# Fused attention and recurrent layer on one core: the odd chunk's levels are made and turned two steps earlier

## The chip, the cores and the metric

The kernel runs on one core of a Trainium2 chip. The metric is the device time in microseconds of one execution. It was measured three times before the change: 699.0, 700.78 and 701.05 us, median 700.78 us.

## What is computed

The input is x of shape (2, 2048, 256), float32: 4096 tokens. The reference is a layer of attention with a hierarchical decay, a layer norm, and then an elementwise recurrent block with a second norm. Its attention part, cut to what matters here:

```python
dl  = (x @ Wdl.T).reshape(B, T, H, LV)              # H = 16 heads, LV = 12 levels
dt  = softplus(x @ Wdt.T + dt_bias)
Lam = softplus(Lp * dl)
cg  = cumsum(-exp(A_log) * dt, axis=1)
decay = exp(where(tril, cg[:, :, None] - cg[:, None], NEG))
lam_ts = Lam taken at level(t, s)                   # level = bit length of t XOR s
Wmat = (Q K^T / 8) * decay * lam_ts
o = (Wmat @ V) @ Wout.T + x ; o = layernorm(o) * ln_g + ln_b
x = layernorm(x + o)
c1 = step(c0, x[0]); c2 = step(c1, x[1])            # gated: f*c + i*g, over the two sequences
x = layernorm(x + tanh(x @ wo.T + c2 @ uo.T + bo))
```

## The kernel before

The 4096 tokens are cut into 32 chunks of 128 tokens, and two chunks make a pair (`sg`, 16 pairs). Everything is written by hand: each engine has its own instruction list, and all the lists walk over the same numbered steps, `STEPS = range(-3, NG + 13)`, with 4 steps to a chunk and so 8 steps to a pair. An engine works through its list strictly in the order in which it is written, and waits on semaphores. At each step an engine issues the jobs that belong to that step. The attention runs in the steps up to about 127 (545 us of the span), the recurrent block (`units_at`) behind it.

What belongs to a pair is scheduled by the table in `token_jobs(s)`: for an entry `(d, j)` the job `j` of pair `sg` falls on step `8 * sg + d - 11`. For the text below these are the jobs that matter, for chunk `ci = 2 * sg` (even) and `ci = 2 * sg + 1` (odd):

- Job 2, step `8 * sg - 10`: `softplus` on GpSimd (L1342), three tensor_tensor and two tensor_scalar over 128x416.
- Job 8, step `8 * sg - 8`: VectorE reads that result and makes `ng`, from which TensorE makes the cumulative sums in `decays`, two steps later.
- Jobs 5 and 7: `levels(sg, c)` on GpSimd (L1376), which writes `AT[c]` and `prod`; job 5 is the even chunk, job 7 the odd one. One step after each, VectorE's `turn_levels(ci)` (L1174) copies four levels into `C`, reduces `prod` into it and transposes `C` into `CT[c]`.
- At step `4 * ci` TensorE's `exponents(ci)` multiplies `AT` and `CT` into the exponents. It also waits until VectorE's `weights` of the chunk before have freed the banks.

Job 2, job 8 and job 7 belong to different pairs at one time: at step `8 * k` VectorE does job 8 for pair `k + 1`, while `exponents` of pair `k`'s odd chunk comes at step `8 * k + 4`.

Per chunk there is a second chain: `turn_y(ci)` (VectorE, L1035, step `4 * ci + 5`) adds the two parts of the result into `yt`, `out_proj(ci)` (TensorE, L501, step `4 * ci + 6`) multiplies it with the output weights, VectorE's `out_proj` (L1086) adds x and takes statistics, GpSimd's `root` (L1393, step `4 * ci + 7`) makes 1/sqrt, VectorE's `normalise` (L1098) and GpSimd's `x1` addition stand at step `4 * ci + 8`. `weights` (L993, tile `W`) multiplies scores and exponentials at steps 1 and 2 of a chunk.

Between these, TensorE runs the three-pass projections of the next pair (tiles `xH`, `xL`, `wH`, `wL`), one piece of 12 matmuls a step. Its list is the same before and after.

Of the kernel before, what the change touches and what calls it, by code (L numbers as in the profile page):

```python
# [45 lines left out]
def token_jobs(s):  # L46

    out = []
    for d, j in ((12, 7), (0, 0), (0, 1), (1, 2), (3, 8), (5, 3), (7, 4), (8, 5)):
        n = s + 11 - d  # L50
        if n % 8 == 0 and (0 if j == 7 else 1) <= n // 8 < NSG:
            out.append((n // 8, j))
    return out
# [16 lines left out]
def misc_jobs(s):  # L70

    out = []
    if 0 <= s < NG:
        ci, cc = s // 4, (s // 4) % CB
        if s % 4 == 0:
            out += [("keys", ci, 0), ("keys", ci, 1)]
        if s % 4 == 1 and cc:
            out += [("inter", ci, 0), ("inter", ci, 1)]
        if s % 4 == 3 and cc < CB - 1:
            out += [("state", ci, 0)]  # L80
    for sg, j in token_jobs(s):
        if j == 3:
            out += [("cgt", sg, 0)]
        if j == 5:
            out += [("cft", sg, 0)]
    for sg, j in token_jobs(s):
        if j == 0:
            out += [("tok", sg, 0), ("tok", sg, 1)]
    return out
# [61 lines left out]
def program(nc, x, xT, wqk, wtok, wout, wffn, cst, bcv, fv, out):  # L151
    ctx = ExitStack()
    with ctx:
# [222 lines left out]
        def _(e):  # L376
# [310 lines left out]
            for s in STEPS:  # L687
# [18 lines left out]
                for sg, j in token_jobs(s):  # L706
                    if j == 3:
                        decays(sg)
# [843 lines left out]
```

How the kernel before makes its waits and increments, by code:

```python
        @block.sync  # L299
# [11 lines left out]
            def load_coefs(sg):  # L311
                m, u = MISC["cft", sg, 0]
                e.wait_ge(m_free[m], u + 1)
                e.dma_start(scr.rearrange("a l c t -> (a l) (c t)"), cT[:, :]).then_inc(l_sc, 16)
                e.wait_ge(l_sc, 16 * sg + 16)
                for c in range(2):
                    ci = 2 * sg + c
                    if ci in INTER:
                        if ci >= 2 and ci - 2 in INTER:
                            for h in range(2):
                                m, u = MISC["inter", ci - 2, h]
                                e.wait_ge(m_free[m], u + 1)
                        for a in range(8):
                            e.dma_start(cB[c][16 * a:16 * a + 16, :, :, :].rearrange("p l u t -> p (l u) t"),
                                        scr[a, :, c, :].partition_broadcast(16)).then_inc(l_cB[c], 16)
# [8 lines left out]
                if i == 2:  # L335
                    e.dma_start(cs[:, :], cst[:, 0:C_CT]).then_inc(l_cst, 16)
                    load_xt(1)
            e.dma_start(C[:, :, :].rearrange("p h l -> p (h l)"), cst[:, C_CT:C_END]).then_inc(l_c, 16)
            e.dma_start(wo[:, :, :], kt(wout)).then_inc(l_wo, 16)
            load_x(0)
            e.dma_start(bv[:, B_G:B_END], bcv[:, B_G:B_END]).then_inc(l_b2, 16)
            e.dma_start(fvs[:, :], fv).then_inc(l_b2, 16)
            load_x(1)
            e.wait_ge(p_proj, 8)
            load_xt(2)
            for sg in range(NSG):
                load_coefs(sg)
```

## Time and profile before

| | before |
|---|---|
| runs, us | 699.0, 700.78, 701.05 (median 700.78) |
| the profiled execution's own time, us | 703.26 |
| its span, first to last instruction, us | 701.5 |
| TensorE busy | 670.3 us, 96% |
| VectorE busy | 475.2 us, 68% |
| GpSimd busy | 355.5 us, 51% |
| ScalarE busy | 339.6 us, 48% |
| mean granted TensorE clock | 0.98 |

Busy time is the time in which an engine had an instruction under way. The ends of matmuls are modelled. The idle time before an instruction is put down to the engine whose semaphore arrived last. The granted clock is the share of full speed (2.4 GHz) that TensorE was given; 0.50 is 1.2 GHz.

### The profile page before, as it was taken

To read this page: it belongs to the slowest core of one execution; us is meant where nothing else is said; L and a number is where in the kernel's file an instruction comes from. 1 tells how busy PE (TensorE), PEld (TensorE's weight loads), DVE (VectorE), ACT (ScalarE), POOL (GpSimd) and SP (SyncE) were. 2 spreads that over 40 slices of the span, in tenths; PEclk is the share of its full clock that TensorE was granted. 3 is DMA by queue.
4 is the path that set the end of the run, shared out by engine and by line. 5 is a ranking of instruction groups with operands and counts; after the bars stand their busy time and mean duration, and the time that the engine had idled before them with its cause. 6 is when DMAs were issued, how large, how long until landed. Compare 5 with 4: busy or idle time off the path is not lost.

```text
span 701.5 us, 22072 instructions
## 1 busy us (share of the span) xinstructions
PE 670.3 (96%) x9172; PEld 603.3 (86%) x9172; DVE 475.2 (68%) x1067; ACT 339.6 (48%) x759; POOL 355.5 (51%) x476
## 2 busy tenths in 40 slices
PE   5889999999999999999999999999997999999994
PEld 3779999998999999899999999999986788888894
DVE  2843768688776968675877769686877445454546
ACT  4545455544444453555444444545443434555555
POOL 1652755645564646466565636565464224344434
PEclk9989999999999999999999999999999899999997
DMA  8020312203050402112150503121222000000002
GB/s 296 26 57 18 80 40 58 68 31 96 3 95 7 92 21 78 35 33 64 35 95 3 95 9 90 35 63 49 35 66 93 1 1 0 31 32 31 30 31 91
DMA packets 53588, 37.09 MB, mean 53 GB/s; under 512 B 5360, under 2 KB 52080, under 8 KB 53488
## 3 DMA queue, kind: packets, MB, share of 16 engines
q1 hardware_dynamic: 53488, 35.67, 20.2%
q8 instruction: 73, 1.20, 0.7%
q14 instruction: 27, 0.22, 0.1%
HBM read 30.41 MB, written 5.24 MB: 51 GB/s over the span
## 4 chain that ended last, share of the span: by engine, by line
PE 88%; DVE 3%; DMA 2%; POOL 2%; ACT 2%; SPq 1%; issue 1%; DVEq 0%; ACTq 0%
PE bank L378 64%; PE bank L381 6%; PE bank L467 5%; PE bank L400 5%; PE bank L432 4%; PE bank L496 4%; SPq L325 1%; DMA xt<-in_wffn 1%; DMA bv<-in_bcv 1%; DVE t L966 1%; ACT t L735 1%; POOL wL L1333 1%; POOL t L1333 0%; DVE ng L963 0%; DVE t L963 0%
## 5 line engine op out<-in xcount | busy, mean ns | idle before, releaser
L378 PE MATMUL bank<-xH,wH 128*128 128x256 f32 x480 | 148.3, 309 | 2.4 <-ACT KT L735 1.1
L378 PE MATMUL bank<-xL,wH 128*128 128x256 f32 x480 | 136.1, 284 | 0.0
L378 PE MATMUL bank<-xH,wL 128*128 128x256 f32 x480 | 135.5, 282 | 0.0
L735 ACT ACTIVATE QT<-bank 128x512 f32<-128x512 f32 x64 | 38.2, 597 | 144.1 <-PE bank L378 144.1
L963 DVE TENSOR_TENSOR W<-bank,E 128x512 f32<-128x512 f32 x128 | 82.2, 684 | 35.6 <-PE bank L378 35.6
L378 PEld LDWEIGHTS bank<-xH,wH 128*128 128x128 f32 x480 | 91.4, 190 | 10.2 <-issue 9.0
L378 PEld LDWEIGHTS bank<-xL,wH 128*128 128x128 f32 x480 | 91.7, 191 | 0.4
L378 PEld LDWEIGHTS bank<-xH,wL 128*128 128x128 f32 x480 | 91.7, 191 | 0.0
L735 ACT ACTIVATE E<-bank 128x512 f32<-128x512 f32 x128 | 66.1, 603 | 17.4 <-PE bank L400 17.4
L378 PE MATMUL bank<-QT,KT 64*128 64x128 f32 x1024 | 65.9, 279 | 0.6 <-ACT E L735 0.6
L735 ACT ACTIVATE KT<-bank 128x512 f32<-128x512 f32 x64 | 38.0, 594 | 54.1 <-PE bank L378 54.0
L378 PEld LDWEIGHTS bank<-QT,KT 64*128 64x128 f32 x1024 | 59.7, 188 | 5.1 <-ACT E L735 0.8
L1333 POOL TENSOR_TENSOR lr<-mv,cs 128x1 f32<-128x1 f32 (+1 forms) x80 | 18.3, 229 | 80.8 <-DVE mv L1116 74.9
L1333 POOL TENSOR_TENSOR rs<-lr,cs 128x1 f32<-128x1 f32 (+1 forms) x80 | 52.4, 655 | 6.3
L1333 POOL TENSOR_TENSOR x<-oo,xs 128x256 f32<-128x256 f32 x32 | 23.5, 735 | 57.8 <-DVE oo L966 57.8
L1333 POOL TENSOR_TENSOR t<-t 128x416 f32<-128x416 f32 x45 | 49.8, 1107 | 3.6
L963 DVE TENSOR_TENSOR g<-g 128x512 f32<-128x512 f32 (+1 forms) x26 | 17.6, 678 | 37.5 <-ACT g L735 37.2
L400 PE MATMUL bank<-CT,AT 32*128 32x128 f32 x1024 | 38.7, 289 | 4.1 <-DVE CT L1188 4.1
L735 ACT ACTIVATE t<-t 128x416 f32<-128x416 f32 x64 | 35.3, 551 | 12.5 <-DVE t L1146 8.1
L1333 POOL TENSOR_TENSOR prod<-ll,cs 128x512 f32<-128x512 f32 x32 | 40.7, 1272 | 0.5 <-DVE ll L963 0.5
L378 PE MATMUL bank<-yH,wH 128*128 128x512 f32 (+1 forms) x102 | 39.8, 390 | 0.0
L400 PEld LDWEIGHTS bank<-CT,AT 32*128 32x128 f32 x1024 | 32.5, 192 | 8.3 <-DVE CT L1188 4.3
(149 smaller groups left out, 1660.5 us busy)
## 6 DMA issues: line engine op xcount, KB each, us to landing
cB<-scr SPq DMA_DIRECT2D x240, 64.0 KB, 3.0
xt<-in_xT SPq DMA_DIRECT2D x16, 256.0 KB, 3.7
xs<-in_x SPq DMA_DIRECT2D x16, 256.0 KB, 4.1
out<-xs SPq DMA_DIRECT2D x16, 256.0 KB, 2.1
xt<-in_wffn SPq DMA_DIRECT2D x8, 256.0 KB, 3.2
QT<-in_wqk SPq DMA_DIRECT2D x4, 256.0 KB, 5.8
KT<-in_wqk SPq DMA_DIRECT2D x4, 256.0 KB, 6.9
scr<-cT SPq DMA_DIRECT2D x16, 64.0 KB, 1.9
```

What stands on the lines that cost most here:

```text
L325: e.dma_start(cB[c][16 * a:16 * a + 16, :, :, :].rearrange("p l u t -> p (l u) t"), scr[a, :, c, :].partition_broadcast(16)).then_inc(l_cB ...
L378: return e.matmul(o, a, b, start=start, stop=stop)
L381: return e.transpose(o, i, ident)
L400: m = e.matmul(XP[q][:, :].rearrange("p (h t) -> p h t", h=H)[:, :, 8 * j:8 * j + 8], AT[b][r, j, :], CT[b][r, :].rearrange("p (h t) -> p ...
L432: y = e.matmul(YB[32 * n:32 * n + 32, 128 * k:128 * k + 128], V[sg % 3][:, c, v:v + 32], W[:, h, :], start=u == 0 and k == 0, stop=u == 1, ...
L467: t = e.matmul(MB[MISC["inter", ci, k][0]][32 * n:32 * n + 32, 128 * i:128 * i + 128], S[r, l, n, 16 * o:16 * o + 32], QT[b][r, 4 * o + n, ...
L496: t = e.matmul(MB[m][k:k + 64, 16 * q:16 * q + 16], Kt[:, 128 * q + k:128 * q + k + 64], Vw[b][:, c, 128 * h + 16 * q:128 * h + 16 * q + 1 ...
L735: return e.activation(o, i, f, **kw)
L963: return e.tensor_tensor(o, a, b, op)
L966: return e.scalar_tensor_tensor(out=o, in0=a, scalar=s, in1=b, op0=op0, op1=op1)
L1333: return e.tensor_tensor(o, a, b, op)
```

## The change

One number of the table moves: job 7 goes from step `8 * sg + 1` to step `8 * sg - 1`. GpSimd's `levels` for the odd chunk is issued there, and VectorE's `turn_levels`, always one step behind it, at step `8 * sg` in place of `8 * sg + 2`. No instruction is added or removed and no DMA moves; the lists of TensorE, ScalarE and SyncE stay as they were.

```diff
 def token_jobs(s):
 
     out = []
-    for d, j in ((12, 7), (0, 0), (0, 1), (1, 2), (3, 8), (5, 3), (7, 4), (8, 5)):
+    for d, j in ((10, 7), (0, 0), (0, 1), (1, 2), (3, 8), (5, 3), (7, 4), (8, 5)):
         n = s + 11 - d
```

First place: VectorE in the last pair that still has a job 8, around step 112. `t3<-pre,t3` is the first instruction of job 8, `oo` are the two of `normalise`, `yt` is `turn_y`. Before:

```order
L963 TENSOR_TENSOR S<-S 128x192
L1120 TENSOR_SCALAR xs<-x1,mv2,rs2 128x256
L966 SCALAR_TENSOR_TENSOR t3<-pre,t3 128x416
L963 TENSOR_TENSOR ng<-t3,eA 128x8x16
L1146 TENSOR_SCALAR t1<-t3 128x416
L1147 TENSOR_SCALAR t4<-pre 128x416
L966 SCALAR_TENSOR_TENSOR oo<-oo,mv1,bv 128x256
L966 SCALAR_TENSOR_TENSOR oo<-oo,rs1,bv 128x256
L963 TENSOR_TENSOR yt<-bank5,zs1 128x256
L963 TENSOR_TENSOR W<-bank1,E 128x512
```

The same place now:

```order
L1120 TENSOR_SCALAR xs<-x1,mv2,rs2 128x256
L1181 COPY C<-ll 128x16x4
L1183 TENSOR_REDUCE C<-prod 128x16x8
L1188 STREAM_TRANSPOSE CT1<-C 128x512
L966 SCALAR_TENSOR_TENSOR t3<-pre,t3 128x416
L963 TENSOR_TENSOR ng<-t3,eA 128x8x16
L1146 TENSOR_SCALAR t1<-t3 128x416
L1147 TENSOR_SCALAR t4<-pre 128x416
L966 SCALAR_TENSOR_TENSOR oo<-oo,mv1,bv 128x256
L966 SCALAR_TENSOR_TENSOR oo<-oo,rs1,bv 128x256
L963 TENSOR_TENSOR yt<-bank5,zs1 128x256
L963 TENSOR_TENSOR W<-bank1,E 128x512
```

The three instructions of `turn_levels` stood behind the chunk's last `W` before; they now stand ahead of job 8, `normalise`, `yt` and all four `W`.

Second place: GpSimd in the same step, as a piece of the difference. `lr1`, `rs1` are `root` of the inner norm, `x1` is the addition behind `normalise`; the five instructions of `softplus` stand directly ahead of this piece in both lists.

```order
 L1333 TENSOR_TENSOR lr1<-mv1,cs 128x1
 L1333 TENSOR_TENSOR rs1<-lr1,cs 128x1
-L1333 TENSOR_TENSOR x1<-oo,xs 128x256
-L1333 TENSOR_TENSOR AT1<-cs,cgt 128x512
-L1333 TENSOR_TENSOR prod<-ll,cs 128x512
+L1333 TENSOR_TENSOR AT1<-cs,cgt 128x512
+L1333 TENSOR_TENSOR prod<-ll,cs 128x512
+L1333 TENSOR_TENSOR x1<-oo,xs 128x256
 L1333 TENSOR_TENSOR lr2<-mv2,cs 128x1
```

`AT1` and `prod` pass the addition `x1` and stand directly behind `root`; `softplus` is still ahead of them.

Third place: the last pair, steps 119 to 121, on GpSimd, where the splits `wL` of the recurrent block's weights stand between.

```order
 L1333 TENSOR_TENSOR rs1<-lr1,cs 128x1
+L1333 TENSOR_TENSOR AT1<-cs,cgt 128x512
+L1333 TENSOR_TENSOR prod<-ll,cs 128x512
 L1333 TENSOR_TENSOR wL<-xt0,wH 128x2x256
 L1333 TENSOR_TENSOR x1<-oo,xs 128x256
 L1333 TENSOR_TENSOR wL<-xt1,wH 128x2x256
-L1333 TENSOR_TENSOR AT1<-cs,cgt 128x512
-L1333 TENSOR_TENSOR prod<-ll,cs 128x512
 L1333 TENSOR_TENSOR lr2<-mv2,cs 128x1
```

Here the two instructions pass two splits and `x1`.

## Rows read from the trace of the kernel before

**Rows 1.** The page: busy time of TensorE; the chain that ended last, by engine.

```profile
PE 670.3 (96%) x9172; PEld 603.3 (86%) x9172; DVE 475.2 (68%) x1067; ACT 339.6 (48%) x759; POOL 355.5 (51%) x476
PE 88%; DVE 3%; DMA 2%; POOL 2%; ACT 2%; SPq 1%; issue 1%; DVEq 0%; ACTq 0%
```

**Rows 2.** Waits, who waited for whom: us in total, times, longest us.

```profile
PE bank L400 <- DVE CT L1188: 4.1, 2, 3.8
PE bank L378 <- DVE ng L963: 3.1, 1, 3.1
...
DVE t L966 <- POOL t L1333: 32.4, 13, 7.9
```

**Rows 3.** Timeline of GpSimd, step 111 to 112: start us, us, instruction, idle time before.

```profile
489.29 3.59 POOL L1333 TENSOR_TENSOR t<-t 128x416 f32<-128x416 f32 x3
...
493.11 0.83 POOL L1333 TENSOR_TENSOR rs<-lr,cs 128x1 f32<-128x1 f32 x1
...
496.18 1.10 POOL L1333 TENSOR_TENSOR AT<-cs,cgt 128x512 f32<-128x512 f32 x1
497.22 1.27 POOL L1333 TENSOR_TENSOR prod<-ll,cs 128x512 f32<-128x512 f32 x1
```

**Rows 4.** Timeline of VectorE, steps 112 to 114.

```profile
492.91 0.59 DVE L966 SCALAR_TENSOR_TENSOR t<-pre,t 128x416 f32<-128x416 f32 x1 [1.04 <-POOL t L1333]
...
495.32 0.42 DVE L963 TENSOR_TENSOR yt<-bank,zs 128x256 f32<-128x256 f32 x1
...
500.46 0.18 DVE L1181 COPY C<-ll 128x64 f32<-128x64 f32 x1
...
501.91 0.39 DVE L963 TENSOR_TENSOR oo<-bank,xs 128x256 f32<-128x256 f32 x1
```

**Rows 5.** Timeline of TensorE, steps 114 and 116: out_proj and exponents.

```profile
497.90 1.03 PE L378 MATMUL bank<-wo,yt 128*128 128x256 f32 x4
...
503.82 1.17 PE L400 MATMUL bank<-CT,AT 32*128 32x128 f32 x32
```

**Rows 6.** Timelines, yt and out_proj of the pairs with the most and the least room.

```profile
271.19 0.42 DVE L963 TENSOR_TENSOR yt<-bank,zs 128x256 f32<-128x256 f32 x1
304.42 0.42 DVE L963 TENSOR_TENSOR yt<-bank,zs 128x256 f32<-128x256 f32 x1
...
274.19 1.03 PE L378 MATMUL bank<-wo,yt 128*128 128x256 f32 x4
306.13 1.03 PE L378 MATMUL bank<-wo,yt 128*128 128x256 f32 x4
```

**Rows 7.** Timelines of GpSimd and TensorE at the start, steps -1 to 2.

```profile
43.78 1.59 POOL L1333 TENSOR_TENSOR prod<-ll,cs 128x512 f32<-128x512 f32 x1
...
45.59 1.06 PE L378 MATMUL bank<-ng,cs 128*128 128x32 f32 x4 [3.05 <-DVE ng L963]
```

**Rows 8.** Timelines of GpSimd, VectorE and TensorE at the end, steps 119 to 124.

```profile
518.79 0.61 POOL L1333 TENSOR_TENSOR rs<-lr,cs 128x1 f32<-128x1 f32 x1
...
521.97 1.28 DVE L963 TENSOR_TENSOR W<-bank,E 128x512 f32<-128x512 f32 x2
524.18 1.02 DVE L963 TENSOR_TENSOR zt<-bank,cB 128x384 f32<-128x384 f32 x2 [0.94 <-PE bank L467]
...
530.03 1.89 PE L400 MATMUL bank<-CT,AT 32*128 32x128 f32 x32 [3.80 <-DVE CT L1188]
```

**Rows 9.** Stretches: us, then busy (instructions) of PE, PEld, DVE, ACT, POOL; PEclk, DMA share, GB/s.

```profile
45.62:55.86 10.24, 10.24 (x80) 9.76 (x84) 6.29 (x14) 2.75 (x5) 1.27 (x1) 0.50 0.01 2
530.31:533.73 3.42, 3.42 (x65) 2.72 (x61) 3.23 (x7) 0.14 (x1) 3.12 (x4) 0.50 0.31 91
690.74:694.15 3.41, 1.20 (x11) 0.99 (x9) 3.31 (x9) 2.82 (x7) 2.84 (x5) 1.00 0.26 88
694.15:697.57 3.42, 0.00 (x0) 0.00 (x0) 2.45 (x9) 2.70 (x7) 2.86 (x7) 0.50 0.33 111
20.50:21.80 1.30, 0.00 (x0) 0.03 (x1) 1.30 (x2) 0.55 (x1) 1.04 (x1) 1.00 0.00 0
```

## The prediction

> **What bounds the kernel now.** I read the page first. TensorE is busy 96% of the span and holds 88% of the chain that ended last, with VectorE at 3% and GpSimd at 2% [rows 1]. So a change on VectorE and GpSimd can only act through TensorE's waits, and the list of waits came next. There the turned levels, which this change moves, cost TensorE 4.1 us in 2 waits, of which one takes 3.8 us; and `ng` costs 3.1 us once [rows 2]. All that an earlier `CT` can remove is therefore 4.1 us. The reader should see the last line of that group too: VectorE itself waits 13 times, 32.4 us in all, for GpSimd's `t`, the end of `softplus`, and it does that exactly at the first instruction of job 8. That is the instruction ahead of which the change puts `turn_levels`.
>
> Then I read the timelines of one pair. GpSimd ends `softplus` at 489.29 + 3.59 = 492.88, makes `lr` and `rs` until 493.94, and only 2.2 us later `AT` and `prod` (496.18 to 498.49) [rows 3]. VectorE starts job 8 at 492.91, directly on `softplus`, ends `yt` at 495.74, and starts the turn at 500.46 [rows 4]. TensorE starts `out_proj`, which reads `yt`, at 497.90, so it has 2.16 us of room, and `exponents` at 503.82, some 1.9 us behind the end of the turn [rows 4, 5]. Nothing waits for `CT` in this pair.
>
> **The change, part by part.** Nothing is added; what matters is what now stands ahead of what.
>
> *The steady pairs.* VectorE's turn needs `prod`, and in GpSimd's list `prod` now stands behind `softplus` and `root`. The reading is: 492.88 (end of `softplus`) + 1.06 (`root`, 492.88 to 493.94) + 2.31 (`AT` and `prod`, 496.18 to 498.49) = 496.25 [rows 3]. VectorE picks it up some 0.04 us later, turns for 1.45 us (500.46 to 501.91) and so begins job 8 at 497.74, not 492.91. From there to the end of `yt` are 2.83 us (492.91 to 495.74), which gives 500.57, and 0.05 us for TensorE to notice: 500.62 [rows 4]. `out_proj` was due at 497.90 [rows 5]. So TensorE stalls for 2.72 us in this pair; put otherwise, `yt` comes 4.88 us later than before and the room of 2.16 us covers part of it. In the other direction, a `root` that runs beside an idle VectorE may take 0.8 rather than 1.06 us, and the shift is then 4.64 us.
>
> Such pairs are those of steps 8, 16, ..., 112: 14. I read `yt` and `out_proj` in each. The room goes from 1.29 us (304.84 to 306.13) to 2.58 us (271.61 to 274.19) [rows 6] (in two of the 14 VectorE comes to job 8 later than `softplus` ends, [rows 2] having 12 waits beside that of the start; one of them has 0.1 us less room, but is also shifted by less). Mean of the 14: 1.96 us. The stall is then between 4.64 - 1.96 = 2.68 and 4.88 - 1.96 = 2.92 us; I take 2.75, near the lower one because of those two pairs: 14 x 2.75 = 38.5 us, bounds 37.5 and 40.9 us. The single ones go from 2.1 to 3.6 us.
>
> Does the delay carry over from pair to pair, or vanish? `softplus` hangs on TensorE's `tokens`, which stands ahead of this `out_proj` in TensorE's list, so a late `out_proj` moves the next `softplus` by the same amount, and the stall comes anew each time. It doesn't grow either: relative to the late TensorE, VectorE is about 2 us behind at `yt`, and gets 1.45 us of that back at once since the turn no longer stands behind the last `W`. `exponents` needs these `W`: they ended at 500.46 before, and 502.5 in the late frame is still ahead of 503.82 [rows 4, 5]. On the queue of GpSimd `x1` is late with `normalise`, and the outer statistics on VectorE stand behind `W` anyway. No DMA and no SyncE work waits for any of it.
>
> *The start.* At step 0 the same happens to the first job 8. `prod` already ends at 43.78 + 1.59 = 45.37, since GpSimd runs ahead. VectorE turns until 46.86, and the two instructions of job 8 up to `ng` take 1.0 us: 47.9, where TensorE started at 45.59 [rows 7]. That is 2.3 us of longer wait. As a bound from below I take 1 us (the part of the slow clock that is then spent waiting), from above 4 us; value 2.
>
> *The end.* Here is what the change can win: the wait of 3.80 us for `CT` at 530.03 [rows 8]. The removed turn (1.45 us) stood directly ahead of it. But `exponents` also needs the last `W`, and VectorE gets to the first `W` later: `rs` ended at 519.40, `prod` (2.31 us) follows at 521.7, the turn at 523.2, `normalise` and `yt` take 1.3 us, so that `W` starts at 524.5 and not at 521.97 [rows 8]. VectorE had 0.94 us of idle time behind it, and loses the rest [rows 8]. 2.5 - 0.94 - 1.45 is about 0. Bounds: -1.5 us (all of the turn) and +1.5 us; value 0.
>
> *TensorE's clock.* The stalls have a second price. The granted clock was 0.50, which is 1.2 GHz, in a stretch of 10.24 us from 45.62 and in one of 3.42 us from 530.31, with TensorE at work in both [rows 9]. The first came behind a wait of 3.05 us, the second behind one of 3.80 us [rows 7, 8]. At the very end TensorE had no work for at most 2.2 us (1.20 us busy in 690.74:694.15) when the clock was 0.50 from 694.15 on. A gap of 1.30 us at 20.50 left the clock at 1.00 [rows 9]. The new stalls lie at 2.1 to 3.6 us, so between a length that did nothing and lengths that did. Half of a slow stretch is lost: 5.1 or 1.7 us. I take 5.1, because behind the first stood the same work as behind the new stalls (projections). For the number of stalls that bring the clock down the bounds are 0 and 14; I take 8, somewhat over half. 8 x 5.1 = 41 us; bounds 0 and 71 us.
>
> The Trainium skill, "TensorE: Matmul & The Clock Gate", section "Why this matters for your kernels", also wants idle gaps between bursts of matmuls avoided, but sets the harmful gap above most of the stalls worked out here. By that rule hardly any of them would bring the clock down, and this term would be near zero.
>
> *Sum.* 703.3 (the profiled execution's own time; its span is 701.5, with 1.8 around it) + 38.5 + 2 + 0 + 41 = 784.8 us. The median of the runs stands 2.5 us under the profiled one: 782 us.
>
> **The rivals.** *The stalls come, the clock holds.* For it: they are mostly shorter than the two waits that were followed by 0.50. Against it: the 2.2 us at the end. Up to 4 falls at 1.7 to 5.1 us belong to it. 703.3 + 38.5 + 2 - 2.5 = 741 us, up to 758. Chance 0.22.
>
> *The clock falls in nearly every pair, or stays down longer.* For it: the slow stretch behind 45.62 lasted until the next `exponents`, and behind the new stalls 5.9 us of full-speed work (497.90 to 503.82) [rows 5] stand ahead of the next `exponents`, 11.8 us at half speed, so that a fall could cost 6 us. 12 x 6 = 72: 703.3 + 38.5 + 2 + 72 - 2.5 = 813 us. Against it: the second fall was over after 3.42 us. Chance 0.15.
>
> *The other side, no stall at out_proj.* This needs `prod` to be there before `softplus` ends, so that VectorE turns in the 1.04 us in which it waits anyway [rows 4]. The place is GpSimd at step `8 * sg - 1`, and it decides whether the shift of `yt` stays under the room of 1.29 to 2.58 us. Then the kernel wins the 1.5 us at the end: 703.3 - 1.5 - 2.5 = 699 us. Against it: GpSimd's list has `softplus` ahead, and 13 times VectorE was already waiting for it [rows 2]. Chance 0.03, and 0.02 for a time within 0.3% of now, where the room would turn out larger than the rows say.
>
> *The change doesn't do what it says*: the two lists in the section on the change show both moves, so I give it nothing of its own.
>
> **How the numbers follow.** The forecast (stalls in all 14 pairs, clock down in 5 to 11 of them) has 0.58 and spans about 755 to 803 us; the held clock has 0.22, the heavier fall 0.15, the two without a stall 0.05. Slower by over 0.3% (what a measurement of this kernel can tell from no change) is 0.95, faster 0.03, same 0.02. The range leaves out the two stall-free cases and the upper part of the heavy one, and starts a little under the 741 of the held clock: 736 to 815 us.
>
> **What would show it.** Right: TensorE waits for VectorE's `yt` some 14 times, 2 to 3.6 us each, near 38 us in all; VectorE waits for GpSimd's `prod`, not `t`, at about 4.4 us a time; the turn starts directly behind it; the wait for `CT` is gone as a name, with `W` or nothing in its place; the start shows a wait of about 5 us for `ng`; the page's clock row has slices under 9, and the clock's mean is near 0.9. Wrong on the clock alone: a mean of 0.97 or more and a time near 741. Wrong altogether: no wait for `yt`, or waits under 1 us each, which would mean that `softplus` or `root` leave GpSimd earlier than I read, or that VectorE makes up for the delay ahead of `yt`.

## The result: 11% slower, and the profile after

The changed kernel takes 774.56 us (median of 6 runs, 772.42 to 777.45), the kernel before 700.91 us (6 runs). The ratio is 1.106, with a 95% interval of 1.102 to 1.109. The prediction said 782 us, between 736 and 815. The profiled executions compared below took 772.42 and 703.26 us of their own, so there are 69.2 us to explain in them.

The page after: busy time, and the granted clock in 40 slices.

```profile
PE 702.4 (91%) x9172; PEld 627.0 (81%) x9172; DVE 471.4 (61%) x1067; ACT 338.1 (44%) x759; POOL 352.5 (46%) x476
PEclk9989999999799999989898989899979789999998
...
PE 47%; POOL 12%; DVE 10%; ACT 3%; issue 3%; DMA 0%; DVEq 0%; POOLq 0%; ACTq 0%
```

TensorE's busy time went up by 32 us with the same matmuls, and the slices of the clock show why: several fell to 7 and 8 tenths. The chain that ended last can here be followed back only to 190.9 us, so its shares add up to 75% of the span. TensorE has 47 of these 75, where it had 88 of 99 [rows 1]. GpSimd and VectorE, 5% together before, have 22: in each of the ten steady pairs that the chain covers it runs through `softplus`, `prod` and the turn.

The waits after (who waited for whom: us in total, times, longest us), against [rows 2]:

```profile
PE bank L378 <- DVE yt L963: 34.7, 15, 3.1
PE bank L378 <- DVE W L963: 6.8, 1, 6.8
PE bank L378 <- DVE ng L963: 5.0, 1, 5.0
PE bank L378 <- DVE zt L963: 3.2, 6, 0.6
PE bank L400 <- DVE W L963: 2.0, 1, 2.0
...
PE bank L378 <- DVE zs L963: 0.6, 2, 0.4
...
DVE C L1181 <- POOL prod L1333: 79.5, 17, 10.2
```

The first line is new and the largest: 15 waits for `yt`, 14 of them in the steady pairs (33.2 us; the fifteenth, 1.5 us, is in the last pair). `ng` has gone from 3.1 to 5.0 us, and the 3.8 us for `CT` have become waits for `yt`, `zt` and `W`. VectorE no longer waits for `t` (32.4 us before) but for `prod`, for 79.5 us.

The same pair as in [rows 3 to 5], on GpSimd:

```profile
550.61 3.58 POOL L1333 TENSOR_TENSOR t<-t 128x416 f32<-128x416 f32 x3
554.15 0.18 POOL L1333 TENSOR_TENSOR lr<-mv,cs 128x1 f32<-128x1 f32 x1
554.41 0.57 POOL L1333 TENSOR_TENSOR rs<-lr,cs 128x1 f32<-128x1 f32 x1
554.95 1.09 POOL L1333 TENSOR_TENSOR AT<-cs,cgt 128x512 f32<-128x512 f32 x1
555.99 1.26 POOL L1333 TENSOR_TENSOR prod<-ll,cs 128x512 f32<-128x512 f32 x1
```

on VectorE:

```profile
557.28 0.20 DVE L1181 COPY C<-ll 128x64 f32<-128x64 f32 x1 [4.11 <-POOL prod L1333]
...
558.74 0.55 DVE L966 SCALAR_TENSOR_TENSOR t<-pre,t 128x416 f32<-128x416 f32 x1
...
561.10 0.42 DVE L963 TENSOR_TENSOR yt<-bank,zs 128x256 f32<-128x256 f32 x1
```

and on TensorE:

```profile
561.57 1.13 PE L378 MATMUL bank<-wo,yt 128*128 128x256 f32 x4 [2.18 <-DVE yt L963]
...
563.19 1.03 PE L378 MATMUL bank<-ng,cs 128*128 128x32 f32 x4 [0.48 <-DVE zt L963]
```

This is the sum of the prediction, link by link. `softplus` ends at 554.19, `prod` at 557.25 (3.06 us later, against 3.37 predicted: `root` is quicker beside an idle VectorE, which the prediction had as its lower bound), the turn takes 1.46 us, and `yt` ends at 561.52, 2.78 us behind the start of job 8 (2.83 predicted). `out_proj` waits 2.18 us, where 4.64 - 2.16 = 2.48 was the lower bound for this pair. The second wait, 0.48 us, was not foreseen: `decays` writes into a bank that `zt` still reads, and `zt` is late with `yt`.

Two stretches after show what the waits do to the clock (columns as in [rows 9]):

```profile
188.50:190.66 2.16, 0.94 (x4) 0.68 (x4) 2.12 (x5) 0.70 (x2) 0.72 (x1) 1.00 0.00 0
190.66:200.90 10.24, 9.95 (x73) 9.25 (x76) 7.21 (x20) 1.49 (x3) 3.31 (x6) 0.50 0.01 2
...
450.07:456.90 6.83, 6.70 (x32) 6.06 (x34) 5.98 (x16) 0.32 (x1) 1.30 (x3) 0.50 0.01 2
```

Behind the waits for `yt`, or already within them, the clock was at 0.50, that is 1.2 GHz, in 10 of the 14 pairs: three times for 3.4 us, five times for 6.8 and twice for 10.2. TensorE was at work for 62 us of these 65, so half of that, 31 us, was lost at first sight.

What the waits cost in all can be read from the starts of `out_proj`. These are its rows for chunk 0 and chunk 28, with the 14 steady pairs between them, first in the kernel before:

```profile
66.72 1.02 PE L378 MATMUL bank<-wo,yt 128*128 128x256 f32 x4
...
513.63 1.03 PE L378 MATMUL bank<-wo,yt 128*128 128x256 f32 x4
```

and in the changed one:

```profile
64.62 1.03 PE L378 MATMUL bank<-wo,yt 128*128 128x256 f32 x4
...
582.44 1.03 PE L378 MATMUL bank<-wo,yt 128*128 128x256 f32 x4
```

The 14 pairs took 446.9 us before and 517.8 us after, 70.9 us more. The stretch ahead of them was 2.1 us shorter in the execution after, and the stretch behind them 0.4 us longer, which gives the 69.2 us.

### The profile page after: what moved, and what is told of

Its sections match the earlier page's. It is cut to its first block, busy times and chain, and to the rows that moved or that the text cites. A ratio compares the mean times of both kernels' runs of the same rounds, so it can differ in the third digit from the quotient of the medians.

```text
span 770.6 us, 22072 instructions
## 1 busy us (share of the span) xinstructions
PE 702.4 (91%) x9172; PEld 627.0 (81%) x9172; DVE 471.4 (61%) x1067; ACT 338.1 (44%) x759; POOL 352.5 (46%) x476
## 4 chain that ended last, share of the span: by engine, by line
PE 47%; POOL 12%; DVE 10%; ACT 3%; issue 3%; DMA 0%; DVEq 0%; POOLq 0%; ACTq 0%
PE bank L378 37%; POOL t L1333 4%; PE bank L381 3%; ACT t L735 2%; PE bank L467 2%; PE bank L496 2%; POOL prod L1333 2%; PE bank L432 2%; POOL t L1346 2%; POOL t L1349 2%; PE bank L400 2%; POOL AT L1333 2%; DVE t L966 1%; DVE W L963 1%; DVE C L1183 1%
## 5 line engine op out<-in xcount | busy, mean ns | idle before, releaser
L378 PE MATMUL bank<-xH,wH 128*128 128x256 f32 x480 | 154.3, 321 | 2.4 <-ACT KT L735 1.1
L378 PE MATMUL bank<-xL,wH 128*128 128x256 f32 x480 | 141.3, 294 | 0.0
L378 PEld LDWEIGHTS bank<-xH,wH 128*128 128x128 f32 x480 | 97.2, 202 | 10.3 <-issue 9.0
L378 PEld LDWEIGHTS bank<-xL,wH 128*128 128x128 f32 x480 | 97.4, 203 | 0.4
L378 PEld LDWEIGHTS bank<-xH,wL 128*128 128x128 f32 x480 | 97.1, 202 | 0.0
L378 PE MATMUL bank<-wo,yt 128*128 128x256 f32 x128 | 40.0, 441 | 34.7 <-DVE yt L963 34.7
L378 PEld LDWEIGHTS bank<-wo,yt 128*128 128x128 f32 x128 | 25.6, 212 | 41.2 <-DVE yt L963 37.9
L1181 DVE COPY C<-ll 128x64 f32<-128x64 f32 x32 | 8.2, 256 | 79.5 <-POOL prod L1333 79.5
L1333 POOL TENSOR_TENSOR Vw<-V,dv 128x128 f32<-128x128 f32 x64 | 24.7, 416 | 39.7 <-ACT dv L735 39.7
L1333 POOL TENSOR_TENSOR xL<-xt,xH 128x512 fp32r<-128x512 f32 x15 | 19.3, 1287 | 49.8 <-ACT xH L735 49.8
```

What stands on the lines that cost most here:

```text
L378: return e.matmul(o, a, b, start=start, stop=stop)
L1181: e.tensor_copy(C[:, :, 24:28], ll[:, c, :].rearrange("p (h l) -> p h l", l=NL)[:, :, 4:8]).then_inc(d_own, 1)
L1333: return e.tensor_tensor(o, a, b, op)
```

## The experiments

**GpSimd's part alone, and job 8 ahead of the turn.** Which of the two engines' orders does it? The first kernel makes `AT` and `prod` early and turns them late:

```diff
-    for d, j in ((12, 7), ...
+    for d, j in ((10, 7), ...
-                for sg, j in token_jobs(s - 1):
-                    if j in (5, 7):
-                        turn_levels(2 * sg + (j - 5) // 2)
+                for sg, j in token_jobs(s - 1):
+                    if j == 5:
+                        turn_levels(2 * sg)
+                for sg, j in token_jobs(s - 3):
+                    if j == 7:
+                        turn_levels(2 * sg + 1)
```

> GpSimd's part of the change alone: AT and prod of the odd chunk are made at step 8k-1, and VectorE's turn stays behind the last W (step 8k+2). My theory (the whole loss comes from yt, which stands behind the turn and so behind prod, on VectorE): 701 us, within 2, TensorE waits for yt never, clock 0.98. Rival (GpSimd's order itself does the harm: x1 now stands behind AT and prod, the outer norm and its statistics come late): TensorE or VectorE waits for x or mv in each of 14 pairs, 710 us or more, up to 774.

Measured: 710.65 us (ratio 1.012, 1.010 to 1.014). My 701 was wrong, and so was the rival's mechanism: neither TensorE nor VectorE waits for `x1` or its statistics. TensorE's waits:

```profile
PE bank L378 <- DVE zt L963: 2.2, 6, 0.5
PE bank L378 <- DVE zs L963: 2.1, 6, 0.4
...
PE bank L378 <- DVE yt L963: 1.0, 2, 0.5
```

VectorE's and GpSimd's timelines in the pair of [rows 3 and 4] show the cause:

```profile
501.17 0.37 DVE L1146 TENSOR_SCALAR t<-t 128x416 f32<-128x416 f32 x1
501.45 1.26 DVE L1147 TENSOR_SCALAR t<-pre 128x416 f32<-128x416 f32 x1
502.63 1.48 DVE L966 SCALAR_TENSOR_TENSOR oo<-oo,mv,bv 128x256 f32<-128x256 f32 x1
504.15 0.48 DVE L966 SCALAR_TENSOR_TENSOR oo<-oo,rs,bv 128x256 f32<-128x256 f32 x1
```

```profile
501.23 1.25 POOL L1336 TENSOR_TENSOR AT<-cs,cgt 128x512 f32<-128x512 f32 x1
502.44 1.39 POOL L1336 TENSOR_TENSOR prod<-ll,cs 128x512 f32<-128x512 f32 x1
```

While GpSimd makes `AT` and `prod`, two VectorE instructions take 1.26 and 1.48 us in place of 0.37 and 0.48: the two engines hinder each other, and `yt` comes 1.9 us later behind the start of job 8 than before. Within this kernel L1147 took 1.27 us the 13 times that it ran beside `AT` or `prod` and 0.36 us the three times that it did not. Before, GpSimd did this work beside `W`, `zt` and `zs`. `W` and `zt` did not suffer; `zs` took 1.08 us in place of 0.43, where nothing waited for it. The late `yt` itself costs TensorE little, since most pairs have 1.8 us of room or more. What costs is `zt` and `zs` behind it, for which `decays` waits: of the 10.4 us that the 14 pairs are longer, 8.3 us lie between an odd chunk's `out_proj` and the next even one. The Trainium skill, "GPSIMD Engine Reference", section "Specifications", says that the two share their SBUF interfaces, with contention where a VectorE instruction has two SBUF inputs or runs in its 2-port mode. These rows agree as far as they go: L966 and `zs`, with two SBUF inputs, were slowed, and `W` and `zt`, which read a PSUM bank and one SBUF tile, were not; in which mode L1147, with one input, ran, no trace shows. In the changed kernel this cost is hidden, because VectorE stands still in these microseconds.

The second kernel is the changed one with `turn_levels` of the odd chunk moved behind `tokens` (job 8), still ahead of `normalise`:

```diff
                 for sg, j in token_jobs(s):
                     tokens(sg, j)
+                for sg, j in token_jobs(s - 1):
+                    if j == 7:
+                        turn_levels(2 * sg + 1)
                 if (ci := chunk_at(s, 8)) is not None:
                     normalise(ci)
```

> As the changed kernel, but in the same step VectorE does job 8 (1.5 us) ahead of the turn, in the time in which it would wait for prod. My theory: yt comes 1.5 us earlier than in the changed kernel, so the wait of TensorE for yt falls from 2.4 to 0.9 us a pair (12 us in all), some 4 us of waits for zt stay, the wait for ng at the start is 3 us again, and waits of 0.9 us leave the clock at 1.00: 717 us. Rival (any stall at this place brings the clock down, whatever its length): the same waits and 31 us of slow clock, 748 us. Rival (the harm is that ng comes late, not yt): 701 us.

Measured: 738.1 us (1.054, 1.048 to 1.060), 21 us above my 717.

```profile
PE bank L378 <- DVE yt L963: 22.1, 15, 2.2
...
PE bank L378 <- DVE zt L963: 3.7, 7, 0.6
PE bank L378 <- DVE ng L963: 3.1, 1, 3.1
PE bank L378 <- DVE zs L963: 2.1, 6, 0.4
```

`ng` is on time and half of the loss is still there, so it is not a late `ng` that counts but `yt`, and `zt` and `zs` behind it. The waits for `yt` in the steady pairs are 1.5 us each, not 0.9. Job 8 now runs beside `root`, `AT` and `prod` and slows them:

```profile
523.61 1.39 POOL L1336 TENSOR_TENSOR prod<-ll,cs 128x512 f32<-128x512 f32 x1
```

Here `prod` ends 3.62 us behind `softplus` (521.38), in the changed kernel 3.06 us. (L1147 took 1.27 us here too, but VectorE then stood still for 1.15 us until `prod` was there, so that cost nothing.) The clock stayed up in 12 of the 14. It fell in two pairs, behind waits of only 1.31 and 1.29 us, each followed by 0.49 us for `zt`, while the longest wait, 2.19 us, left it alone.

**The waits filled.** How much of the loss is the clock? The changed kernel and the kernel before got 14 more matmuls ahead of `out_proj`:

```diff
             def out_proj(ci):
+                if ci % 2 and 1 <= ci <= 27:
+                    e.wait_ge(a_qk, 8 * ((ci + 1) // 2 + 1) + 3)
+                    for _ in range(14):
+                        mm(banks[0][:, 0:256], wtH[:, 0, 0:128], wtH[:, 0, 0:256])
                 e.wait_ge(d_yt, ci + 1)
```

> The changed kernel with TensorE kept at work in its stalls: ahead of the odd chunks' out_proj in the 14 steady pairs it does 14 more matmuls of 128x256 (1.7 us in all, results never read) into the bank of the projections, once ScalarE has emptied it (about 0.8 us). My theory (the changed kernel loses some 37 us in waits and some 30 us by the clock that falls behind them): the waits are filled, the clock stays near 1.00 in the steady pairs, 743 us, up to 748 where the work is longer than the stall. Rival (the clock costs nothing of its own, since slow stretches only use up room that TensorE has): 774 us or a little more.

> The kernel before with the same 14 more matmuls at the same place, 14 times. There they fill no stall: each costs 1.7 us and about 0.8 us of waiting for ScalarE, 2.5 us x 14 = 35 us, 736 us, clock 0.98. It is the price of delaying out_proj by about as much as the change does, at full clock. If it comes near the filled changed kernel, the delay and the clock are all that the change does. A rival in which the shifted order on VectorE and GpSimd costs by itself has the filled changed kernel 10 us or more above it.

Measured: 772.11 us (1.099, 1.096 to 1.102) for the changed kernel, 737.57 us (1.052, 1.049 to 1.054) for the kernel before. The control came as expected: 36 us for 14 delays of 2.6 us at full clock, and no new fall of the clock in the steady pairs. The changed kernel stayed 34.5 us above it, which by the expectation would speak for a cost of the shifted order by itself; but this run did not test what it should:

```profile
PE bank L378 <- ACT QT L739: 26.9, 14, 2.6
```

The added matmuls waited 2 us for ScalarE themselves, so the gap stayed open and the work came on top. ScalarE's copy of `QT` stands behind its own part of job 8 (`Ln` of `t`), which waits for VectorE:

```profile
561.27 0.55 ACT L739 ACTIVATE t<-t 128x416 f32<-128x416 f32 x1 [4.72 <-DVE t L1150]
561.73 0.58 ACT L739 ACTIVATE QT<-bank 128x512 f32<-128x512 f32 x1
```

That is a second way by which a late job 8 reaches TensorE, hidden behind `yt` in the changed kernel. The rival's number was met for a reason that is not the rival's.

So the work was put where it waits for nothing, 18 matmuls (2.1 us) ahead of the projection one step earlier:

```diff
                 e.wait_ge(a_qk, 8 * sg + j)
+                if j == 2 and sg >= 2:
+                    for _ in range(18):
+                        mm(banks[0][:, 0:256], wtH[:, 0, 0:128], wtH[:, 0, 0:256])
```

> The changed kernel with 18 more matmuls of 128x256 (2.1 us, results overwritten) ahead of the projection of step 8k+1 in the 14 steady pairs, so that TensorE reaches the late out_proj 2.1 us later and waits there for 0.2 to 1 us only; unlike in the first filled kernel the added work waits for nothing of ScalarE. My theory (about 40 us of the change's cost are waits, about 30 us the slow clock behind them): the delay of yt stays, the clock stays at 1.00 in the steady pairs, 744 us, within 5. Rival (the slow clock costs nothing, since the next wait takes up what it loses): 774 us.

Measured: 751.31 us (1.071, 1.066 to 1.076): more work, and 23 us less time, though 7 us above my 744, because the delay is longer than the 40 us that I had put. Waits, and the steady pairs in one stretch:

```profile
PE bank L378 <- DVE yt L966: 5.1, 8, 1.5
...
PE bank L378 <- DVE zt L966: 3.6, 7, 0.6
PE bank L378 <- DVE zs L966: 2.1, 6, 0.4
```

```profile
60.00:572.00 512.00, 498.68 (x7917) 453.27 (x7915) 349.22 (x811) 226.58 (x537) 257.37 (x346) 1.00 0.20 48
```

The changed kernel, in the same stretch:

```profile
60.00:572.00 512.00, 472.51 (x7151) 428.19 (x7133) 333.80 (x781) 212.09 (x502) 245.84 (x329) 0.94 0.20 45
```

The clock was 1.00 in the steady pairs, and the delay stayed. Its size is read again from `out_proj` of the chunks 0 and 28:

```profile
67.50 1.02 PE L378 MATMUL bank<-wo,yt 128*128 128x256 f32 x4
...
560.54 1.03 PE L378 MATMUL bank<-wo,yt 128*128 128x256 f32 x4
```

The 14 pairs took 493.0 us, 46.1 us more than before and 24.8 us less than in the changed kernel. So 46 us are the delay at full clock and 25 us the clock, not quite the 31 of the halved stretches (the medians of the runs differ by 23.3 us). Pair by pair, the two kernels agree within 0.05 us in the four pairs in which the changed kernel's clock held. In the other ten a slow stretch of 3.4 us cost it 1.0 to 1.5 us, one of 6.8 us 2.3 to 2.7 us, and one of 10.2 us 4.2 or 4.3 us. One reason that it is less than half is in the waits: for `zt` and `zs` they are 5.7 us here against 3.8, so a slow clock uses up some room that TensorE else waits out.

**Is it the turn, or the prod it waits for?** Here the turn stays first in step `8 * k`, but `prod` has two buffers, and GpSimd makes both chunks' levels ahead of `softplus`:

```diff
-        prod = sb1("prod", [P, H, 8, 4])
+        prod = [sb1(f"prod{i}", [P, H, 8, 4]) for i in range(2)]
...
-                    if j in (5, 7):
-                        levels(sg, (j - 5) // 2)
+                    if j == 5:
+                        levels(sg, 0)
+                        levels(sg, 1)
...
```

(Chunk 1's levels are made ahead of the loop, and the waits for `prod` are adapted.)

> VectorE's turn stays where the change puts it, first in step 8k, but prod has a buffer for each chunk, and GpSimd makes both chunks' AT and prod at step 8k-3, ahead of softplus. My theory (the harm is the wait for a prod that stands behind softplus, 4.4 us a pair; the turn's own 1.45 us fit into the 1 to 3 us in which VectorE waits for softplus anyway): TensorE waits for yt in no pair or for tenths, 702 us, within 3. Rival (the 1.45 us of the turn ahead of job 8 do the harm): 14 stalls of 1.4 us or more, 725 us or more. A cost I can't see from here: AT and prod beside VectorE's work at step 8k-3 may slow that by about 1 us a pair, which would show as a later softplus, up to 710 us.

Measured: 701.41 us, ratio 1.001 (0.999 to 1.004): the whole loss is gone with VectorE's order as the change has it, the clock held in all 14 pairs, and they took 1.4 us longer than before. VectorE waits 9 times for `softplus` and not 13 times as in [rows 2], which fits a turn that fills some of that time:

```profile
DVE t L966 <- POOL t L1333: 14.1, 9, 5.2
```

**The two ends apart.** The table has both entries for job 7, and one pair takes the new one:

```diff
-    for d, j in ((12, 7), (0, 0), ...
+    for d, j in ((12, 7), (10, 7), (0, 0), ...
-        if ... (0 if j == 7 else 1) <= n // 8 < NSG:
+        if ... (0 if j == 7 else 1) <= n // 8 < NSG and (j != 7 or (d == 10) == (n // 8 == 15)):
```

> The change in the last pair alone (k = 15, steps 119 and 120). In the changed kernel the waits at this place came to 4.0 us (yt 1.5, zt 0.5, W 2.0) where the kernel before has 3.8 (CT) and 0.6 (E). My theory: the removed turn is paid back by the later W, 701 us, within 1.5. Rival (the earlier CT does win its 1.5 to 3.8 us here): 697 to 699 us.

> In the last pair GpSimd makes AT and prod at step 119 as in the changed kernel, but VectorE turns them behind the first two W of chunk 30 (step 121), where it had 0.94 us of idle time in the kernel before. My theory: of the 1.45 us of the turn 0.9 disappear in that gap, so exponents start some 0.9 us earlier; with a wait of 2.9 us in place of 3.8 us the clock may also stay up, which gives 1.7 us more. 699.5 us, between 698 and 701. Rival (AT and prod beside normalise slow VectorE by 1.9 us as in the kernel with GpSimd's part alone, and eat it): 701 us or more.

> The change in the first pair alone (k = 0, steps -1 and 0). In the changed kernel the wait for ng there was 5.0 us in place of 3.1 us, and the slow clock began inside that wait. My theory: 1.9 us more waiting, 0 to 2.7 us less slow clock at work: 701 us, within 2. Rival (the start belongs to the loss with 3 to 4 us of its own, since a longer wait brings a longer slow stretch): 704 us or more.

(The second has `turn_levels` of the last chunk behind the first two `W` of chunk 30, the third has 0 in place of 15.) Measured: the last pair alone has ratio 0.9998 (0.998 to 1.002), the variant in the gap 1.0004 (0.999 to 1.002), the first pair alone 1.0038 (1.002 to 1.006), 2.7 us. So nothing is won at the end, by either way, and my 699.5 for the gap was wrong where its rival was right: in the last-pair kernel `exponents` waited 2.20 us for `W` behind 1.5 us for `yt` and 0.5 for `zt`; in the gap variant `AT` and `prod` ran beside `normalise`, whose two instructions took 1.47 and 1.38 us, and ate the gap. At the start the interval is 1.1 to 4.2 us, against the 1.9 us by which the wait for `ng` is longer in the changed kernel; whether it costs more than this wait is not shown.

**A version of the kernel before with an earlier first `prod`.** The start has the same hindrance in the kernel before: job 8 ran beside `AT` and `prod`, 2.7 us up to `ng`.

```diff
             decayed_values(0)
+            levels(0, 1)
             for s in STEPS:
```

(with two `prod` buffers, and chunk 1 left out of job 7.)

> The kernel before with one thing changed: GpSimd makes AT and prod of chunk 1 ahead of the first softplus of the loop, where it waits 3.4 us for ScalarE, into a second prod buffer; VectorE's order is that of the kernel before. My theory: job 8 at the start no longer runs beside AT and prod, so that VectorE's two instructions up to ng take 1.0 us and not 2.7 us, TensorE waits 1.3 us and not 3.1 us for ng (as in the kernel with a second prod), 699.3 us, and up to 3 us less where the clock then stays up. Rival (softplus comes later by the 2.4 us of AT and prod): 701 us or more.

Measured: 700.81 us, ratio 0.998 (0.996 to 0.9994). It is the fastest kernel of the study, by 0.2%, at the edge of what the runs can tell: 0.4 to 2.9 us, in which the 1.8 us of the shorter wait for `ng` lie.

```profile
41.80 0.59 DVE L966 SCALAR_TENSOR_TENSOR t<-pre,t 128x416 f32<-128x416 f32 x1 [7.93 <-POOL t L1333]
42.43 0.37 DVE L963 TENSOR_TENSOR ng<-t,eA 128x128 f32<-128x128 f32 x1
```

TensorE waited 1.3 us for `ng`, not 3.1 us. The clock fell all the same, for 6.8 us.

## Why the prediction was right, and where its sizes were off

**The mechanism** held in the steps that it had, and lacked one path (below): `prod` behind `softplus` on GpSimd, the turn behind `prod`, job 8, `normalise` and `yt` behind the turn, and one stall of `out_proj` per pair that does not add up from pair to pair. The kernel with two `prod` buffers shows that the wait for `prod` is the cause; the same 1.45 us of the turn at the same place cost nothing without it.

**The stalls**: predicted 38.5 us, measured 33.2 us of idle time shown (14 waits of 1.80 to 3.09 us, mean 2.37). A part of the difference is in how waits are shown: matmuls of a projection start every 0.12 us but are drawn 0.28 us long, so that a gap behind them appears 0.16 us shorter than it is. By the starts of `out_proj`, the odd one came 35.5 us later behind the even one, summed over the 14 pairs. Most of the remaining 3 us is the quicker `root`.

**A term that was missing**: the prediction follows the delay on VectorE to `yt`, `W`, `x1` and the statistics, but not to `zt` and `zs`, which stand behind `yt`. It hits `decays` too, through the bank that they read: 8 waits, 3.8 us as shown. At full clock, in the filled kernel, the stretch from an odd `out_proj` to the next even one grew by 10.2 us over the 14 pairs, and 9.2 us of that is `decays`, which starts up to 0.8 us later behind `out_proj`. So the prediction's nothing was 10 us.

**The clock**: predicted 41 us from 8 falls of 5.1 us. There were 10 falls, but TensorE's work in them was 6.2 us each (31 us in all when halved), and the filled kernel puts the real price at 25 us, 2.5 us a fall. The step that was mis-sized is taking the 10.24 us stretch of [rows 9] as the typical one: it was the longest kind, two of ten. The prediction cites the Trainium skill, "TensorE: Matmul & The Clock Gate", section "Why this matters for your kernels", which wants no idle gaps above some 3 us between bursts of matmuls. The trace does not agree that shorter ones are safe: the waits of 2.5 to 3.1 us brought the clock down in 7 of 7 pairs, six of them with waits under 2.8 us, and those of 1.8 to 2.2 us in 3 of 7.

**The start**: 2 us predicted, 2.7 us (1.1 to 4.2) measured for it alone. In the two profiled executions compared here the changed kernel was even 2.1 us ahead at the first `out_proj`, because two things at the start were shorter: its first wait for `W` (6.8 us, before 8.5) and its slow stretch (6.8 us, with 4.85 us of work in it, against the 10.24 us of [rows 9]). **The end**: 0 predicted, 0 measured; the removed wait for `CT` turned into waits for `yt`, `zt` and `W` of 4.0 us in all.

The sum of what was measured between the profiled executions: 35.5 for `yt`, 10.2 for `decays`, 24.8 for the clock, -2.1 for the start and 0.4 for the end, 68.8 of the 69.2 us. Of the predicted 81.5 us the clock had 16 too many and `decays` 10 too few. That the time came within 8 us of the forecast is thus in part luck: two wrong sizes stood against each other.

## What to carry to other kernels

Moving a producer and its consumer "two steps sooner" gives slack only if the resource that the producer needs is free there: look at what stands ahead of it in its engine's list, and at what the consumer now stands ahead of. When an in-order engine is already waiting at the place of insertion, as the wait of [rows 2] said here, anything put in front that depends on the same busy engine turns that free wait into a longer one. Follow the delay to everything that stands behind it in that list, also to reads that only free a bank: here they were 10 of 46 us. And price a new stall of TensorE twice, once for the gap and once for the clock behind it; filling the gap with useless matmuls gave back a third of the loss here.

## What the runs showed of the hardware that was not expected

- The length of a gap alone did not decide whether TensorE's clock fell. A wait of 1.3 us followed by 0.49 us brought it down in two pairs, waits of 2.19 us and 1.90 us in the same kernel did not; in the changed kernel 2.07 us did it in one pair and not in another. Slow stretches lasted 3.4, 6.8 or 10.2 us.
- A VectorE TENSOR_SCALAR over 128x416 took 0.37 us alone and 1.26 us beside GpSimd's TENSOR_TENSOR over 128x512, a SCALAR_TENSOR_TENSOR over 128x256 0.48 and 1.48 us. In the kernel with GpSimd's part alone such overlaps cost 8 to 9 us, without any new dependency.
